# Context tiles of batches 2 to 16 turned by VectorE's 32x32 blocks and a turn through DRAM, in place of TensorE's transposes

## The reference

```
x = x + cross_attention(layernorm(x), ctx)      # 16 heads of 64, rope on the keys, logits clipped to +-11
    lat = layer_norm(x, lat_g, lat_b);  c = layer_norm(ctx, ctx_g, ctx_b)
    q = lat @ Wq;  k, v = split(c @ Wkv);  k = rope(k, cos, sin)
    out = softmax(clip(q k^T / 8)) v @ Wo + bo
x = x + linear_attention(layernorm(x))          # 16 heads of 16, relu features, cumulative sums
x = x + experts(layernorm(x))                   # top 2 of 8 experts, 256 -> 1024 -> 256
```

## Time and profile before

| | |
|---|---|
| median of 3 runs | 1257.02 us |
| profiled execution | 1255.76 us, span 1254.0 us, granted clock 0.998 |
| PE busy | 1226.5 us (98%) |
| DVE busy | 936.9 us (75%) |
| ACT busy | 704.7 us (56%) |
| POOL busy | 678.9 us (54%) |
| DMA | 149.95 MB, mean 120 GB/s |
| steps of the cross attention | about 51.5 to 980 us of the span |

### The profile page before, as it was taken

The page is one execution under the profiler, slowest core; times in us unless marked ns, Lnnn a source line. Parts: engine busy times, 40 slices in busy tenths (PEclk is TensorE's granted clock), DMA queues, the critical chain, the costliest instruction groups (busy, mean ns, idle before and its releaser), DMA issues.

```text
span 1254.0 us, 40596 instructions
## 1 busy us (share of the span) xinstructions
PE 1226.5 (98%) x16508; PEld 1027.6 (82%) x16508; DVE 936.9 (75%) x1924; ACT 704.7 (56%) x1359; POOL 678.9 (54%) x611
## 2 busy tenths in 40 slices
PE   7999999999999999999999999999999999999997
PEld 3678888888888888888888888888888788789997
DVE  6797877777887777877777787777777356768886
ACT  7756556555655655655655665665643233356664
POOL 3466666666576566566566566666554123333333
PEclk9999999999999999999999999999999999999999
DMA  6345444545445445445444444444545261566662
GB/s 235 66 99 114 99 107 110 107 100 114 101 98 114 104 108 115 103 98 113 105 106 105 108 101 105 111 106 102 132 99 130 88 219 36 187 178 194 205 186 73
DMA packets 96913, 149.95 MB, mean 120 GB/s; under 512 B 29452, under 2 KB 64728, under 8 KB 96600
## 3 DMA queue, kind: packets, MB, share of 16 engines
q1 hardware_dynamic: 92648, 143.14, 46.2%
q0 software_dynamic: 4080, 4.22, 1.7%
HBM read 66.20 MB, written 14.83 MB: 65 GB/s over the span
## 4 chain that ended last, share of the span: by engine, by line
PE 92%; ACT 2%; DVE 2%; DMA 2%; issue 1%; POOL 1%; SPq 0%; POOLq 0%; ACTq 0%; DVEq 0%
PE bank L1421 30%; PE bank L1451 28%; PE bank L1407 11%; PE bank L1759 6%; PE bank L1476 3%; PE bank L1431 2%; PE bank L1587 2%; PE bank L1809 2%; PE bank L1811 1%; PE bank L1810 1%; PE bank L1616 1%; PE bank L1659 1%; PE bank L1510 1%; DMA w_two<-in_L_ffn_W_dram 1%; PE bank L1640 1%
## 5 line engine op out<-in xcount | busy, mean ns | idle before, releaser
L568 POOL TENSOR_TENSOR kr<-kr,ksw 128x1024 f32<-128x1024 f32 x128 | 308.7, 2412 | 341.7 <-DVE pr L969 219.3
L1421 PE MATMUL bank<-ct,wk_hi 128*128 128x512 f32 x1024 | 331.7, 405 | 0.0
L1451 PE MATMUL bank<-p_hi,xc 128*128 128x512 f32 x1024 | 315.8, 390 | 0.0
L720 ACT ACTIVATE ctf<-bank,vecs 128x128 f32<-128x128 f32 x256 | 103.3, 453 | 333.5 <-PE bank L1431 333.5
L1451 PEld LDWEIGHTS bank<-p_hi,xc 128*128 128x128 f32 x1024 | 191.9, 188 | 39.9
L1421 PEld LDWEIGHTS bank<-ct,wk_hi 128*128 128x128 f32 x1024 | 182.3, 188 | 41.8
L1421 PE MATMUL bank<-ct,wk_lo 128*128 128x512 f32 x512 | 200.6, 392 | 0.0
L1451 PE MATMUL bank<-p_lo,xc 128*128 128x512 f32 x512 | 200.5, 392 | 0.0
L1001 DVE TENSOR_TENSOR kw<-bank,stab 128x512 f32<-128x512 f32 x256 | 175.7, 686 | 27.7 <-PE bank L1421 24.8
L992 DVE TENSOR_TENSOR p_lo<-pr,p_hi 128x1024 fp32r<-128x1024 f32 x128 | 184.3, 1440 | 1.8 <-ACT p_hi L707 1.8
L1009 DVE TENSOR_TENSOR ct<-ctf,ct 128x256 fp32r<-128x256 f32 x128 | 57.8, 452 | 170.6 <-ACT ct L725 170.6
(11 more groups left out here) (215 smaller groups left out, 1728.8 us busy)
## 6 DMA issues: line engine op xcount, KB each, us to landing
ksw<-kw SPq DMA_DIRECT2D x512, 128.0 KB
raw<-in_ctx_dram SPq DMA_DIRECT2D x64, 256.0 KB, 4.0
w_two<-in_L_ffn_W_dram SPq DMA_DIRECT2D x15, 1024.0 KB, 5.1
x_slots<-fill SPq DMA_DIRECT2D x128, 64.5 KB, 2.9
w_all<-in_L_ffn_W_dram SPq DMA_DIRECT2D x4, 2048.0 KB, 17.6
wo<-in_L_ffn_W_dram SPq DMA_DIRECT2D x7, 1024.0 KB, 5.2
lsum<-l_rows SPq DMA_DIRECT2D x64, 64.0 KB, 2.7
xs<-x_slots SPq DMA_DIRECT2D x23, 129.0 KB, 2.2
```

Source lines behind the costliest of these rows:

```text
L568: pool.tensor_tensor(kr[:, i], kr[:, i], ksw[:, i], ALU.add).then_inc(kr_done, 1)
L720: last = act.activation(ctf[:, k], psT[:, k * P:(k + 1) * P], ACT.Identity, bias=vecs[:, 3, k:k + 1], scale=vecs[:, 2, k:k + 1])
L1421: last = pe.matmul(psK[:, a * 512:(a + 1) * 512], l[:, k, w], ct[:, h % 3, r, k], start=(m == 0), stop=(m == len(parts) - 1))
L1451: last = pe.matmul(psZ[c], xc[:, slot_, l, t, cols], r[:, i, :, t], start=(f == 0 and m == 0), stop=(f == 1 and m == len(parts) - 1), skip ...
```

## The change

For the first batch (8 tiles) nothing changes in kind. For the other 120 tiles PE no longer turns the tile. DVE transposes the tile in blocks of 32x32 into a new buffer xt (`blocks_turned`, after p_lo in each step). When a half's four tiles are there, SP writes xt to DRAM in four DMAs (x_turned, one per 32 partitions, in pieces of 128 elements), behind the key exchange of a step with j mod 4 = 1, and in the next step, ahead of that step's exchange, reads it back in one DMA into ctf with partitions and columns in place. ACT then applies gain and bias in place on ctf (two activations of 512 columns) and casts the high part, DVE makes the low part; both at the end of the step with j mod 4 = 2. Both xt and ctf are single buffers, now of a half each. In ct the columns of a half now stand in the order (block of 32, tile, row), which the rope products undo as they read psK. Statistics and normalisation run two steps further ahead. To make room in memory some late loads move: Wout, bo and bout are loaded in step 118 (STEPS - 10), and vbd is cleared in step 120 on POOL.

```diff
+        with ExitStack() as turning:
+            xt = sb("xt", [P, D // HALF, HT, HALF], F32, turning)
+            ctf = sb("ctf", [P, KC, HALF_S], F32, turning)
...
+        x_turned = nc.dram_tensor("x_turned", [KC, P, HALF_S], F32, kind="Internal").ap()
...
+        def tile_cols(whole, t):
+
+            return whole.rearrange("p k (i t s) -> p k i t s", t=HT, s=HALF)[:, :, :, t]
+
+        def by_tile(whole):
+
+            return whole.rearrange("p (t i s) -> p t i s", t=HT, s=HALF)
...
+                if due(j, 2) and (j + 6) // 4 < 2 * B:
+                    h = (j + 6) // 4
+                    sp.wait_ge(xt_moved, 80 * (h - 2) + 64)
+                    wait(sp, ct_lo_done, HT * h)
+                    sp.dma_start(ctf[:], x_turned.rearrange("c p s -> p c s")).then_inc(xt_moved, 16)
...
+                if due(j, 1) and (j + 7) // 4 < 2 * B:
+                    h = (j + 7) // 4
+                    sp.wait_ge(xt_done, HT * (h - 1))
+                    wait(sp, xt_moved, 80 * (h - 2))
+                    for i in range(4):
+                        sp.dma_start(x_turned[:, :, i * P:(i + 1) * P].rearrange("c (k p) s -> p (c k) s", p=HALF),
+                                     xt[i * HALF:(i + 1) * HALF].rearrange("p k t s -> p k (t s)")).then_inc(xt_moved, 16)
...
-                if j >= 0 and j % 2 == 0 and j // PAIRS + 2 < B:
-                    sp.wait_ge(xT_ps, j + 2)
-                    sp.wait_ge(x_lo_done, j + 2)
-                    context(j // PAIRS + 2, j % PAIRS // 2)
+                if j >= -2 and j % 2 == 0 and (j + 2) // PAIRS + 2 < B:
+                    if j + 2 < ST:
+                        sp.wait_ge(xT_ps, j + 4)
+                    else:
+                        sp.wait_ge(xt_done, j + 4 - ST)
+                    sp.wait_ge(x_lo_done, j + 4)
+                    context((j + 2) // PAIRS + 2, (j + 2) % PAIRS // 2)
...
+                if j == STEPS - 10:
+                    for r in range(KC):
+                        for h in range(2):
+                            sp.dma_start(wout_raw[:, r, h * P:(h + 1) * P].rearrange("p (g d) -> p g d", d=AD),
+                                         Wout[r * P:(r + 1) * P, :].rearrange("p (g h d) -> p h g d", h=2, d=AD)[:, h]).then_inc(wout_ld, 16)
...
-                if there(j + 11) and j + 11 >= ST:
-                    i = (j + 11) % 2
-                    pool.wait_ge(stats_done, j + 12)
-                    pool.tensor_tensor(ve[:, i:i + 1], mv[:, i, 1:2], consts[:, 3:4], ALU.add).then_inc(var_done, 1)
-                    pool.wait_ge(var_done, j + 12)
+                if there(j + 13) and j + 13 >= ST:
...
+                if j == STEPS - 8:
+                    pool.wait_ge(ct_lo_done, TILES)
+                    pool.memset(vbd[:], 0.0).then_inc(vbd_ones, 1)
...
-                if there(j + 9):
+                if 0 <= j + 9 < ST:
                     n, t = tile_at(j + 9)
                     act.wait_ge(xT_ps, j + 10)
-                    wait(act, ct_lo_done, j + 9)
                     for k in range(KC):
-                        last = act.activation(ctf[:, k], psT[:, k * P:(k + 1) * P], ACT.Identity, bias=vecs[:, 3, k:k + 1], scale=vecs[:, 2, k:k + 1])
+                        last = act.activation(tile_cols(ctf[:], t)[:, k], psT[:, k * P:(k + 1) * P].rearrange("p (i s) -> p i s", s=HALF), ACT.Identity,
+                                              bias=vecs[:, 3, k:k + 1], scale=vecs[:, 2, k:k + 1])
                     last.then_inc(ctf_done, 1)
-                    if t == 0 and j + 9 >= 3 * HT:
-                        act.wait_ge(k_ps, 2 * last_key((j + 9) // HT - 3) + 2)
                     act.wait_ge(ctf_done, j + 10)
-                    act.copy(ct[:, n, 0, :, t * P:(t + 1) * P], ctf[:]).then_inc(ct_hi_done, 1)
+                    act.copy(tile_cols(ct[:, n, 0], t), tile_cols(ctf[:], t)).then_inc(ct_hi_done, 1)
+                if due(j, 2) and (j + 6) // 4 < 2 * B:
+                    h = (j + 6) // 4
+                    act.wait_ge(xt_moved, 80 * (h - 1))
+                    for k in range(KC):
+                        last = act.activation(ctf[:, k], ctf[:, k], ACT.Identity, bias=vecs[:, 3, k:k + 1], scale=vecs[:, 2, k:k + 1])
+                    last.then_inc(ctf_done, 1)
+                    if h >= 3:
+                        act.wait_ge(k_ps, 2 * last_key(h - 3) + 2)
+                    act.wait_ge(ctf_done, ST + h - 1)
+                    act.copy(ct[:, h % 3, 0], ctf[:]).then_inc(ct_hi_done, HT)
...
+            def blocks_turned(j):
                 if ST <= j + 11 and there(j + 11):
-                    i = (j + 11) % 2
-                    dve.wait_ge(bn_done, j + 12)
-                    dve.bn_aggr(mv[:, i], bst[:, i]).then_inc(stats_done, 1)
+                    n = j + 11
+                    dve.wait_ge(xhat_done, n + 1)
+                    if n % HT == 0:
+                        wait(dve, xt_moved, 80 * (n // HT - 3) + 64)
+                    dve.transpose(xt[:, :, n % HT], raw[:, n // ST % 2, n % ST].rearrange("p (k s) -> p k s", s=HALF)).then_inc(xt_done, 1)
...
-                    dve.tensor_tensor(kw[:, i, cols], psK[:, cols], stab[:, places], ALU.mult).then_inc(kw_done, 1)
-                    dve.tensor_tensor(kr[:, i, cols], psK[:, cols], ctab[:, places], ALU.mult).then_inc(ku_done, 1)
+                    keys_ = psK[:, cols].rearrange("p (i t s) -> p t i s", t=HT, s=HALF)
+                    dve.tensor_tensor(by_tile(kw[:, i, cols]), keys_, by_tile(stab[:, places]), ALU.mult).then_inc(kw_done, 1)
+                    dve.tensor_tensor(by_tile(kr[:, i, cols]), keys_, by_tile(ctab[:, places]), ALU.mult).then_inc(ku_done, 1)
...
+                    dve.tensor_tensor(tile_cols(ct[:, n, 1], t), tile_cols(ctf[:], t), tile_cols(ct[:, n, 0], t).bitcast(F32), ALU.subtract).then_inc(ct_lo_done, 1)
+                if due(j, 2) and (j + 6) // 4 < 2 * B:
+                    h = (j + 6) // 4
+                    dve.wait_ge(ct_hi_done, HT * (h + 1))
+                    dve.tensor_tensor(ct[:, h % 3, 1], ctf[:], ct[:, h % 3, 0].bitcast(F32), ALU.subtract).then_inc(ct_lo_done, HT)
...
+                blocks_turned(j)
...
             def turn_context(j):
-                if there(j):
+                if 0 <= j < ST:
                     pe.wait_ge(xhat_done, j + 1)
                     wait(pe, ctf_done, j)
-                    if due(j - 9, 7):
-                        pe.wait_ge(o_sum, (j - 16) // 4 * 2 + 1)
```

More of the change, by code:

```diff
@@ L91, in build @@
         feat_w = sb("feat_w", [P, 2, P])
-        with ExitStack() as middle:
-            vbd = sb("vbd", [P, 2, AH, 2 * (AD + 1)], F32, middle)
-        h_lo_0 = sb("h_lo_0", [P, 2 * AH * 2 * (AD + 1)], F32R)
         square = sb("square", [P, P])
@@ L538, in _ @@
             pool.memset(cvec[:, 1:2], EPS)
-            pool.memset(vbd[:], 0.0).then_inc(vbd_ones, 1)
-            pool.wait_ge(vbd_ones, 1)
-            for b in range(2):
-                at = b * (AD + 1) + AD
-                pool.memset(vbd[b * N:(b + 1) * N, :, :, at:at + 1], 1.0).then_inc(vbd_ones, 1)
-                pool.wait_ge(vbd_ones, b + 2)
             for c in range(2):
@@ L937, in normalised @@
             def normalised(j):
-                if 0 <= j + 10 < ST:
-                    n = j + 10
-                    dve.wait_ge(rstd_done, n + 1)
+                for n in range(max(j + 11, 0) if j > -10 else 0, min(j + 12, ST)):
+                    dve.wait_ge(rstd_done, (n // HT + 1) * ST)
                     dve.tensor_scalar(raw[:, 0, n], raw[:, 0, n], xl_mom[:, n, 0:1], xl_rsd[:, n:n + 1], ALU.subtract, ALU.mult).then_inc(xhat_done, 1)
             def shifts(j):
-                if ST <= j + 10 and there(j + 10):
-                    i = (j + 10) % 2
-                    dve.wait_ge(rstd_done, j + 11)
-                    if j + 10 >= ST + 2:
-                        dve.wait_ge(xhat_done, j + 9)
+                if ST <= j + 12 and there(j + 12):
+                    i = (j + 12) % 2
+                    dve.wait_ge(rstd_done, 2 * (j + 13))
+                    if j + 12 >= ST + 2:
+                        dve.wait_ge(xhat_done, j + 11)
                     dve.scalar_tensor_tensor(out=shift[:, i:i + 1], in0=mv[:, i, 0:1], scalar=-1.0, in1=rstd[:, i:i + 1],
@@ L952, in counted @@
             def counted(j):
-                if ST <= j + 11 and there(j + 11):
-                    n = j + 11
+                if ST <= j + 13 and there(j + 13):
+                    n = j + 13
                     b, t = n // ST, n % ST
```

77 lines of the change are left out of this document (41 added, 36 removed).

## The result

The changed kernel takes 1375.8 us (median of 4 runs, 1368.0 to 1376.1) against 1258.9 us for the kernel before beside it (1255.8 to 1261.5): 1.092 times as long, 95% interval 1.089 to 1.094. It is slower by 117 us. The forecast was 1326 us with a range of 1283 to 1385; the sign, the place of the loss and the range held, the size was 50 us short.

The account below looks back on a forecast made before the run. PE, busy for 98% of the span, was taken as the bound. From the profiled 1255.76 us, -37.2 for transposes and +106.7 for the stall gave 1325.3, plus 1.3 to the runs' median: 1326 us, range 1283 to 1385.

Parts of the forecast that it names:

- The transposes: On PE: two transposes fewer in each of 120 tiles, 0.31 us a pair, 37.2 us saved.
- The stall: DVE's first transpose of a half waits for the writes from xt, delaying PE's scores: 3.68 us, 29 times, 107 us.
- L: Time from the last write's issue to its landing in DRAM, taken as 3.5 us; the stall is L + 0.18.
- The DVE transpose: One DVE transpose of 256 columns added a step, taken as 0.34 us.
- The read-back: The 512 KB load of a half, taken as 4.6 us: just fits, over 5.1 us it becomes a second stall.
- The clock: PE's granted clock, said to stay at 1.00 in the forecast as summed.
- rival 3: PE's clock falls after each stall: 1.65 us more, 29 times, 48 us, giving 1374 us; 15%.
- the likeliest case: The forecast as summed, with the stall and the clock at 1.00: 55%, its own range 1283 to 1344 us.
- C to D: PE's scores of the step with j mod 4 = 3 to those with 0; before the change at 420.21 and 428.30.
- The ends: First eight tiles and late loads moved to the last steps: put at zero, within 4 us either way.
- Rival 1: At the same DVE transpose: the wait is hidden and the gain stays, 1220 us; 8%.
- Rival 2: The read-back stalls as well: each us over 5.1 costs 30 us, at 6.1 us the time is 1356; 18%.

Follow-up runs that it names:

- e1: The kernel before without PE's transposes of tiles 8 and up; ACT reads the unturned tile, no DVE transpose, no DRAM: 1230.1 us, ratio 0.979.
- e2: The changed kernel with the four writes reading a constant weight tile instead of xt, so DVE need not wait for them: 1369.3 us, ratio 1.089.
- e8: The changed kernel with only ACT's and DVE's work on the read-back half moved one step later: 1390.3 us, ratio 1.104.
- e4: The changed kernel with 20 unread matmuls of 256 columns on PE ahead of the scores of steps with j mod 4 = 3: 1353.8 us, ratio 1.078.
- e3: The changed kernel with the four writes ahead of the key exchange of the same step instead of behind it: 1270.2 us, ratio 1.012.
- e7: The changed kernel with the read-back behind its step's exchange, and each half's first DVE transpose and the work on the half one step later: 1282.3 us, ratio 1.018.
- e9: The changed kernel with SP's order changed: writes before the exchange, read-back right behind it, a context load put off behind the read-back: 1246.5 us, ratio 0.9913.
- e10: e9 with the first DVE transpose of each half one step later: 1245.9 us, ratio 0.9907.
- e5: e3 with the first DVE transpose of each half put off to the next step: 1285.5 us, ratio 1.019.
- e6: e5 with ACT's and DVE's work on the read-back half moved one step later: 1291.1 us, ratio 1.026.

## Why the forecast was short, step by step

- **The transposes: 37.2 us forecast, about 30.5 measured**. The start-to-start distance was read rightly and was the wrong quantity: some 0.09 us of it belong to the first 64x64 matmul behind the pair and stay without the pair (e1). Off by 6.7 us.
- **The stall: 106.7 us forecast, 103.4 measured** (PE idle ahead of the scores 105.6 us, less 2.2 in the kernel before). DVE's waits are 29, as forecast, and 103.4 us over 29 is 3.57 us each for 3.68. That it comes out so close is luck in part, for two errors cancel in it. From the first issue of the exchange to DVE's start it is 7.66 us in the mean of 29 halves, and the forecast had 418.75 - 411.10 = 7.65. But L, from the start of the last write's issue, is 3.0 us of it in the mean (2.7 in the median, forecast 3.5), and the issues take the rest: 2.75 + 1.94 us from the exchange's first to the last write's, forecast 2.37 + 1.78 by the median of one issue, though the four exchange issues of that very step had taken 3.14 us; in the period shown one issue among the writes was slow (3.36 us for the four). With the median of L alone the forecast would have been near 1303.
- **The DVE transpose: 0.34 us forecast, 0.37 measured start to start** (0.435 busy), from a row of its size; the 0.62 us that two of the bf16 figure of the Trainium skill (VectorE: DVE Perf Modes, "The three transpose paths") would make does not hold for it. The rope products stayed at 0.69 us and less.
- **The read-back: it fitted, as computed, but only behind the first stall.** ACT waits 10.1 us in all. Its activations of 512 columns took 0.81 us for 0.57 forecast, which was read from a copy out of PSUM. The Trainium skill (ScalarE: Activation LUTs, What ACT_TABLE_LOAD costs) gives 280 ns with a pointer as bias, 93 for a second pointer and 0.833 ns a column: 0.80 us, and the trace agrees (0.807 us in the median). DVE's low part took 1.67 us in the median for 1.29. e2 shows that this chain is itself 2.9 us late once the first wait is gone.
- **The clock: the forecast said 1.00 and had the fall as rival 3, at 15% and 48 us; it came.** This is the step of the likeliest case that failed, and the largest part of what was missing: the sentence that a fall needs the stall to be long enough, "and here work surrounds it". Work on both sides of a stall of 3.6 us does not protect the clock. The fall in the earlier trace rows, after a stretch in which PE was busy for half the time, was the better guide. C to D takes 9.01 us in the mean for 7.69 at full clock, 29 times: 38 us. The priced 1.65 us a time was for a full stretch at half clock with every instruction doubled; 1.32 was the measure, with half clock in 24 places for 29 stalls.
- **The ends: 0 forecast, 8 us measured.** The first scores start at 54.23 for 51.53 us and the tail is 5.6 us longer, a stretch of it at half clock:

```profile
1110.00:1125.00 15.00, 12.27 (x131) 10.44 (x130) 6.14 (x22) 3.65 (x8) 1.43 (x3) 0.66 1.01 327
```

  e1 has 2.0 and 3.5 us of them without any of the moved loads. The clock has a part in the tail. From the last scores to the end it is 281.8 us in the kernel before, where the clock is at half only in the last few us; with 3.4 us more at half clock it is 282.4 and 285.2 (e8, e4), with 6.8 us 284.6 to 286.2 (e2, e3, e7, e9, e10), with 10.2 us 285.3 to 286.7 (e1, e5, e6) and with 13.7 us 287.4 (here). Why the clock falls there, and what makes the 2 to 3 us at the start, was not tried.

The sum of the measured terms: -30.5 + 103.4 + 38 + 8 = 119 of the span's 120.0 us. The forecast's terms were +69.5; the clock makes 38 of the missing 50, the transposes 7, the ends 8, and the stall gives 3 back.

Rival 1 (the wait is hidden and the gain stays) is right in what it says of the place: e9 moves the last write ahead of the exchange, and the gain comes back, 10.6 us of it. It was rightly given little for this kernel, in which the writes stood behind the second kw. Rival 2 (the read-back stalls as well) did not come, since the first stall covers it.

## What to carry to other kernels

A stall in a loop on an engine that was fully busy has two prices: itself, and the clock behind it; where a forecast has a stall like this one (some 3.5 us in each turn of a loop), the fall belongs in the likeliest case, not in a rival. A DMA queue is a program in its own order: before a transfer is priced by its landing, look at which waits stand ahead of it in the queue, since moving four issues over one block was worth over 100 us here, while in e9 all that the change adds, transfers included, costs some 16 us over e1. And when a wait is taken away in a thought, walk on to the next wait of the same loop: two that hide each other give nothing one at a time (1369 and 1390 us) and most of the loss together (1282 us).

## What the runs showed of the hardware that was not expected

- Leaving out two 128x128 transposes between 128-row matmuls and 64x64 tiles gives back 0.227 us, not the 0.31 us from their start to the next matmul's: a transpose costs 0.109 us, and the first 64x64 matmul starts some 0.09 us later than one of the same kind would, with the pair (0.202 us for 0.109) and without it (0.318 for 0.227).
- Dead matmuls in a gap pay: 20 of 256 columns, 2.55 us of PE, made the kernel some 20 us faster, with 5 stretches at half clock among the steps for 24.
- Writing 128 KB to DRAM in pieces of 512 bytes lands 2.6 us after its issue in the median, and a read of 512 KB 3.5 us: less than the 4.0 us of the 256 KB context load. Behind the exchanges in e7 they take 3.0 and 4.6 us.
- A VectorE transpose in 32x32 blocks of 256 fp32 columns takes 0.435 us, no more than a plain operation of that size.
